# Weighted sums of the odd token tiles' expert outputs moved from VectorE to GpSimd in a four-layer transformer kernel

## What is computed

```python
# layer 2: 32 experts, 4 per token
topk_w, topk_idx = jax.lax.top_k(probs, 4); topk_w = topk_w / sum(topk_w)
act = jax.nn.silu(g) * u
eo = jnp.einsum('tei,eih->teh', act, w_down)
routed = jnp.einsum('te,teh->th', combine, eo)
...
# layer 3: 16 experts, 2 per token
for e in range(16):
    y = y + (silu(xf @ W1[e] + b1[e]) * (xf @ W11[e] + b11[e]) @ W2[e] + b2[e]) * gates[:, e, None]
```

## Time and profile before

| | us |
|---|---|
| median of 3 runs (lowest, highest) | 1688.22 (1686.22, 1691.62) |
| the profiled execution, its own time | 1694.55 |
| its span in the trace | 1692.7 |
| DVE busy in the span | 1250.0 (74%) |
| PE busy | 1260.5 (74%) |
| POOL busy | 412.5 (24%) |
| combine stage of layer 2: first gather issued, last combine begun | 1098.49, 1217.90 |
| combine stage of layer 3, the same | 1608.36, 1663.30 |

### The profile page before, as it was taken

The page is one execution under the profiler, slowest core; times in us unless marked ns, Lnnn a source line. Parts: engine busy times, 40 slices in busy tenths (PEclk is TensorE's granted clock), DMA queues, the critical chain, the costliest instruction groups (busy, mean ns, idle before and its releaser), DMA issues.

```text
span 1692.7 us, 24051 instructions
## 1 busy us (share of the span) xinstructions
PE 1260.5 (74%) x7110; PEld 675.0 (40%) x7198; DVE 1250.0 (74%) x4139; ACT 910.8 (54%) x2172; POOL 412.5 (24%) x578
## 2 busy tenths in 40 slices
PE   6988979887422333246678999977899888999976
PEld 2444544444111111131135656513366344666621
DVE  5998979989789999868656566667766865555672
ACT  3898988887254444411344565544444444455454
POOL 0111202002000000003556345265310153232160
PEclk7999989999755555555789999978899999999998
DMA  3010100100293000012332566333211026547220
GB/s 114 26 68 8 49 27 26 55 0 1 80 330 116 3 9 11 1 39 90 114 99 83 180 186 191 100 86 67 55 32 31 35 79 159 158 123 179 98 69 21
DMA packets 141387, 135.41 MB, mean 80 GB/s; under 512 B 75218, under 2 KB 114455, under 8 KB 141203
## 3 DMA queue, kind: packets, MB, share of 16 engines
q1 hardware_dynamic: 126185, 101.99, 20.6%
q0 software_dynamic: 13440, 31.48, 6.1%
q10 hardware_dynamic: 1632, 0.39, 0.1%
HBM read 95.96 MB, written 47.27 MB: 85 GB/s over the span
## 4 chain that ended last, share of the span: by engine, by line
PE 45%; DVE 33%; ACT 9%; issue 8%; another core or an unknown queue 2%; DMA 2%; SPq 1%; POOL 0%; DVEq 0%; ACTq 0%
PE PS L577 40%; DVE RA L1733 6%; DVE nmx L1488 5%; DVE RA L1737 4%; PE PS L573 4%; DVE RA L1291 3%; DVE RA L1294 2%; ACT RA L1879 1%; ACT RA L1929 1%; DVE RB L1291 1%; DVE RB L1294 1%; DVE X L1475 1%; DVE Otok L1218 1%; ACT RB L1885 1%
## 5 line engine op out<-in xcount | busy, mean ns | idle before, releaser
L577 PE MATMUL PS<-RA 128*128 128x512 bf16 (+6 forms) x1961 | 508.3, 352 | 102.4 <-DVE nmx L1488 64.6
L1488 DVE TENSOR_REDUCE nmx<-PS 128x1 f32<-128x512 f32 x512 | 347.2, 686 | 237.2 <-PE PS L577 210.0
L1929 ACT ACTIVATE RA<-PS 128x512 f32<-128x512 f32 x512 | 301.1, 599 | 214.9 <-PE PS L577 151.4
L577 PEld LDWEIGHTS PS<-RA 128*128 128x128 bf16 (+4 forms) x2048 | 200.7, 121 | 356.3 <-issue 142.1
L577 PE MATMUL PS<-RA,Vs 128*32 128x512 f32 x1240 | 204.1, 654 | 5.1 <-ACT RA L1929 1.0
L2055 ACT ACTIVATE RA<-RA 128x8 f32<-128x8 f32 x511 | 107.5, 210 | 143.0 <-DVE RA L1733 142.7
L573 PE MATMUL PS<-ident,RB 128*128 128x128 f32 (+2 forms) x331 | 62.7, 334 | 158.5 <-DVE RB L1666 142.9
L1908 ACT ACTIVATE RA<-PS 128x256 f32<-128x256 f32 (+1 forms) x144 | 55.0, 382 | 171.7 <-PE PS L577 158.3
L1291 DVE TENSOR_SCALAR RA<-PS 128x1024 f32<-128x1024 f32 x96 | 117.0, 1219 | 20.9 <-PE PS L577 20.6
L1879 ACT ACTIVATE RA<-RA,nm 128x512 f32<-128x512 f32 x192 | 128.8, 725 | 0.9 <-POOL nm L2225 0.7
L1294 DVE CUSTOM_DVE_ANT_0 RA<-RA,RB 128x512 f32<-128x512 f32 x192 | 125.1, 689 | 3.3
(11 more groups left out here) (312 smaller groups left out, 2127.1 us busy)
## 6 DMA issues: line engine op xcount, KB each, us to landing
RA<-scr SPq DMA_DIRECT2D x288, 96.0 KB
RA<-wd SPq DMA_DIRECT2D x28, 384.0 KB
xd<-Otok SPq DMA_DIRECT2D x36, 256.0 KB, 3.3
RA<-xd POOLq DMA_DIRECT2D x72, 128.0 KB, 3.8
RA<-wd SPq DMA_DIRECT2D x56, 160.0 KB
RB<-wd SPq DMA_DIRECT2D x20, 384.0 KB
RB<-wd SPq DMA_DIRECT2D x40, 160.0 KB
scr<-parts SPq DMA_DIRECT2D x48, 128.0 KB
```

What stands on the lines that cost most here:

```text
L577: return e.matmul(o, l, r, start=first, stop=last)
L1488: e.tensor_reduce(nmx[:, (g + lx) % 3, c:c + 1], bank[(6, 0)[i % 2]], AX.X, ALU.max, negate=True).then_inc(*ROWMAX.up(layer, n, i))
L1929: e.activation(chunk(layer, k, i), bank[(1, 5)[i % 2]], ACT.Exp).then_inc(*EXP.up(layer, k, i))
```

## The change

The combines of the odd tiles (n = 1, 3, ..., 15) are done by GpSimd; those of the even tiles stay on VectorE as they are. GpSimd has no single operation for it here, so it multiplies the gathered slot in place by the weight (a tensor_scalar) and, after a wait for its own result, adds the product to X[:, n] (a tensor_tensor). A new semaphore, `XR`, counts GpSimd's combines; `writer` picks `XW` or `XR` by the tile's parity wherever somebody waits for a combine: the gather i for slot i-6, VectorE's statistics and its later additions to X, the first row loads of layer 3, and the stores of the output. GpSimd keeps a `written` table of its own.

```diff
+    def writer(n, event):
+
+        return XR if event[0] == "routed" and n % 2 else XW
...
         def x_last(n):
             if n in written:
-                dve.wait_ge(XW, *written[n])
+                dve.wait_ge(writer(n, written[n]), *written[n])
...
             elif name == "combine":
                 i = task[1]
                 n, j = i // topk[lx], i % topk[lx]
-                dve.wait_ge(GATH[i % 6], lx, i)
-                x_last(n)
-                dve.wait_ge(ROUTE, "done", lx)
-                e.scalar_tensor_tensor(out=X[:, n, :], in0=XG[:, i % 6 // 2, i % 2, :], scalar=WJ[:, n, j:j + 1], in1=X[:, n, :],
-                                       op0=ALU.mult, op1=ALU.add).then_inc(*XW.up("routed", lx, i))
+                if n % 2 == 0:
+                    dve.wait_ge(GATH[i % 6], lx, i)
+                    x_last(n)
+                    dve.wait_ge(ROUTE, "done", lx)
+                    e.scalar_tensor_tensor(out=X[:, n, :], in0=XG[:, i % 6 // 2, i % 2, :], scalar=WJ[:, n, j:j + 1], in1=X[:, n, :],
+                                           op0=ALU.mult, op1=ALU.add).then_inc(*XW.up("routed", lx, i))
                 written[n] = ("routed", lx, i)
...
                 if i >= 6:
-                    pool.wait_ge(XW, "routed", lx, i - 6)
+                    pool.wait_ge(writer((i - 6) // k, ("routed",)), "routed", lx, i - 6)
...
+            elif name == "combine":
+                i = task[1]
+                n, j = i // k, i % k
+                if n % 2:
+                    pool.wait_ge(GATH[i % 6], lx, i)
+                    pool.wait_ge(writer(n, written[n]), *written[n])
+                    pool.wait_ge(ROUTE, "done", lx)
+                    y = XG[:, i % 6 // 2, i % 2, :]
+                    e.tensor_scalar(y, y, WJ[:, n, j:j + 1], None, ALU.mult).then_inc(*XR.up())
+                    pool.wait_last(XR)
+                    e.tensor_tensor(X[:, n, :], X[:, n, :], y, ALU.add).then_inc(*XR.up("routed", lx, i))
+                written[n] = ("routed", lx, i)
```

More of the change, by code:

```diff
@@ L268, in build @@
     XG_A, YO_A = signal("act_xg"), signal("act_yo")
-    ROOT = signal("pool_root")
+    ROOT, XR = signal("pool_root"), signal("pool_routed")
     SET, PARTS_P, BIAS_P, NEGMAX = signal("pool_set"), signal("pool_parts"), signal("pool_bias"), signal("pool_negmax")
@@ L2074, in pool_program @@
         e = pool.e
+        written = {}
         def early3(name, b, *more):
@@ L2149, in expert_step @@
                 if i >= 6:
-                    pool.wait_ge(XW, "routed", lx, i - 6)
+                    pool.wait_ge(writer((i - 6) // k, ("routed",)), "routed", lx, i - 6)
                 e.indirect_dma_start(XG[:, i % 6 // 2, i % 2, :], None, yd[lx],
                                      bass.IndirectOffsetOnAxis(ap=IDX[:, n, j:j + 1], axis=0)).then_inc(*GATH[i % 6].up(lx, i))
+            elif name == "combine":
[10 more added lines that the diff above has]
+                written[n] = ("routed", lx, i)
+            elif name == "down":
+                written[shared[lx][task[1]][0]] = ("shared", lx, task[1])
         def scatter(lx, i):
@@ L2165, in first_rows @@
             if lx:
-                pool.wait_ge(XW, "routed", 0, 16 * topk[0] - 1)
+                pool.wait_ge(XR, "routed", 0, 16 * topk[0] - 1)
             for u in range(6):
@@ L2209, in beside_step @@
                 biases()
+            for task in side[layer].get((n, i), ()):
+                if task[0] == {2: "proj2", 3: "proj"}[layer]:
+                    for tile in range(4 * task[1], 4 * task[1] + 4):
+                        written[tile] = ("x", layer, task[1])
         e.memset(Vs[:, :, :, :], 0.0).then_inc(*SET.up("vs"))
@@ L2475, in sp_program @@
             sp.wait_ge(XW, "shared", 1, 8 * b + 7)
-            sp.wait_ge(XW, "routed", 1, 8 * b + 7)
+            sp.wait_ge(XW, "routed", 1, 8 * b + 5)
+            sp.wait_ge(XR, "routed", 1, 8 * b + 7)
             e.dma_start(out[b].rearrange("(n p) d -> p n d", p=128), X[:, 4 * b:4 * b + 4, :]).then_inc(*STORE.up("all"))
```

## The result

The changed kernel took 1704.97 us (median of 5 runs, 1702.55 to 1708.44), the kernel before 1688.22 (5 runs, 1684.98 to 1691.62): a ratio of 1.0087, 95% interval 1.0068 to 1.0105; the medians differ by 16.8 us. I had forecast 1690.1 and no measurable change. The measured median lies 2 us above the upper end of my range, 1703 (by the ratio, 1.0087 x 1688.22 = 1702.9, it lies at that end), and comes out near the rival "GpSimd bounds both stages" (1701.0). The profiled execution took 1708.44 us, with a span of 1706.6.

A forecast was written before the change was run, and what follows sets the result against it. TensorE and VectorE bound the kernel by handing PSUM banks to and fro; with the change GpSimd bounds layer 3. Layer 2 -2.5, layer 3 +2.4 and blocking +2 gave +1.9 us on 1688.22: 1690.1, range 1681 to 1703.

The forecast's parts named there:

- GpSimd bounds both stages: Layers 2 and 3: at 1.2 us a combine GpSimd's queue costs +4.2 and +6.6, blocking 2: 1701.0 us; chance 0.22.
- the price of GpSimd's multiply: GpSimd's odd combines: a 128-column multiply takes 286 ns, drawn from the slope of its one-input casts.
- The two-level picture: Both combine stages: GpSimd works in order, and VectorE's even combine i waits for gather i to land.
- layer 3 has no room: Layer 3's stage: gather 29 lands at 1662.5, after combine 29's former 1660.10; +2.4 us, VectorE's gain not seen.
- the 2 of blocking: VectorE operations beside GpSimd's combines hold each other up; +2 us on the chain, between 0 and 4.
- The pair 0.85: GpSimd's multiply and add lengthen the distance of two gathers by 0.85 us, from 0.70 and two waits of 0.07.
- Landing: Both stages: a gather takes at most 4.4 us from issue to landing; 4.4 was taken.
- The burst wait: Layer 2: gathers 10 and 11 come behind combines 4 and 5, so VectorE waits 1.9 us at combine 11.
- VectorE's relief: Layer 2: 32 fewer combines on VectorE give 5.1 us, the chain's figure, capped at 4.9 by gather 59.
- The statistics: VectorE's statistics that wait for GpSimd's combines have one to two steps of room; 0.5 us put on them.
- the lock: Both engines' combines coincide by rhythm; half of 96 operations wait 0.2, 9.6 us on the chain: 1697.7 us; chance 0.08.
- What would show it: Signs in the changed trace: GpSimd nearly never idle, VectorE waiting before even combines, combine 59 earlier, combine 29 later.

The follow-up runs named there:

- its halves: Two kernels, GpSimd doing odd combines in only one layer, against the kernel before (1642.50 us): layer 2 only 1665.44 us, layer 3 only 1658.67 us.

## Why the prediction's mechanism held and its size did not

The forecast was +1.9 us and no measurable change; +16.8 was measured. That the range nearly reaches this is owed to its upper end, where every term stood at its largest together, and not to the sum. The step that failed is the price of GpSimd's multiply, and the smaller ones follow it.

- **The two-level picture** (GpSimd works in order, a gather behind its combines, an even combine behind its gather) was right, and so was the claim that layer 3 has no room. The rival's 1701.0 came from 1.2 us a combine; 1.24 was measured, 0.04 x 26 + 0.04 x 12 = 1.5 us more. The prediction's own working with 1.24 in the place of 0.85 lands gather 59 at 1215.5 and gather 29 at 1667.2, +5.2 and +7.1 us, with the 2 of blocking +14.3.
- **The multiply was mis-sized, and this decided the sign.** I drew 286 ns for 128 columns from a cast's slope between 512 and 1024 columns; it took 626, and 574 with a constant. The fit was right for what it fitted: the trace of before has casts of 128x128 at 288 and 291 ns. Wrong was to carry it over to another operation. That trace also had a float32 tensor_scalar of GpSimd, which I didn't read, with two columns only:

```profile
L2219 POOL CAST identb<-ident 128x128 bf16<-128x128 f32 x1 | 0.3, 288 | 0.0
L2225 POOL TENSOR_SCALAR nm<-mx 128x2 f32<-128x2 f32 x128 | 27.3, 213 | 319.0 <-DVE mx L1294 255.4 <-ACT RA L1879 55.1 <-ACT RB L1879 8.6
```

  It gives no price for 128 columns by itself, but 213 ns for two left only 73 for the other 126 in a price of 286. The add was right: 430 drawn from the slope, 450 to 476 measured. Of the seams 0.02 and 0.19 were taken, 0.04 and 0.27 measured. The pair 0.85, measured 1.24, over my own limit of 1.04 for a net loss in layer 2. The nearest whole row, the power operation's 0.96, lay nearer than the fit by chance only: it is one operation over 4 columns, not a pair over 128.
- **Landing.** I took 4.4 us. Gather 10 landed at most 4.38 us behind its issue (1115.30 to 1119.68), gather 11 5.67 (1117.80 to 1123.47), gather 29 of layer 3 2.67 (1670.79 to 1673.46). The burst wait that I had named, at combines 10 and 11, came, at 4.4 us for 1.9, and a third one of 5.3 which I had not. The nine waits of layer 3 (14.6 us) are the bound that I had forecast there.
- **VectorE's relief** was put at 5.1 us, capped at 4.9, and didn't show where the combines were dropped (ratios 1.0027 and 1.0022). It may be part of the 6 us by which the kernel that only adds beat the kernel before; no run tells the relief from the spacing of the gathers. The earlier trace rows gave 10.0% of the chain to "another core or an unknown queue", and I read past it. Half of a chain's share is what a cut gives only if nothing stands ready behind it.
- **The statistics** got 0.5 us. They waited three times, 9.4 us, once for 5.74:

```profile
1137.68 0.29 DVE L1538 BATCH_NORM_STATS2 st<-X 128x6 f32<-128x128 f32 x1 [5.74 <-POOL X L2169]
```

  They read a block of four tiles right behind its last, an odd one, so they meet GpSimd's row at its latest point. With the multiply doubled it was 8.99. That this is a cost on top of the row isn't shown: VectorE would have waited for a landing soon after.
- **Blocking** was put at 2 us and is of that size. The kept combines have 356 ns instead of 342 on average, some 0.49 beside GpSimd's work (1119.68 above), and GpSimd's add went up to 1.25 beside an operation of VectorE over 1024 columns with two inputs in SBUF:

```profile
1161.99 1.22 DVE L1191 TENSOR_TENSOR parts<-QK,parts 128x1024 bf16<-128x1024 f32 x1
1162.28 1.25 POOL L2169 TENSOR_TENSOR X<-X,RA 128x128 f32<-128x128 f32 x1
```

  A gather's issue beside another such operation (1157.01) took 1.63 us for 0.95. Over the stages that makes 48 x 0.014 = 0.7 us on VectorE, and 48 x (0.476 - 0.45) = 1.2 on GpSimd, the engine that bounds, if all of the difference is blocking. The rule of the Trainium skill (SBUF — State Buffer, Who interferes with whom), as the prediction has it, agrees in kind with these rows; what it cost is about a tenth of the loss. One of the prediction's rows was misread: the 0.17 us "where nothing ran beside it" (795.76) ran beside GpSimd's cast of 795.61 to 795.89, so it shows a tensor_scalar that a cast did not hold. The rival "the lock" (9.6 us) is not what happened.
- **What would show it**, in its own words: GpSimd busy to the end (102.1 of 128.2 us, before 66.2 of 119.4) and VectorE waiting before combines 10 and 11 were seen; combine 59 "two to three us earlier" was 9.1 later, combine 29 "some 2 later" 6.0. The granted clock fell from 0.87 to 0.84 in 40 us of layer 2's stage, with TensorE 29.5 instead of 31.6 us busy, and over the whole stages from 0.84 to 0.81 and from 0.91 to 0.86. All three signs that I had named for being wrong came: the pair over 1.0, the statistics waiting several us, the clock outside 0.87 to 0.89. The stretches, as in the earlier trace rows, and the two stages:

```profile
1140.00:1180.00 40.00, 29.54 (x140) 12.05 (x135) 27.48 (x70) 15.95 (x34) 33.04 (x40) 0.84 0.30 62
1097.80:1226.00 128.20, 89.66 (x415) 30.41 (x423) 79.35 (x212) 50.48 (x99) 102.09 (x127) 0.81 0.29 69
1615.80:1676.00 60.20, 43.13 (x195) 11.05 (x197) 35.06 (x83) 26.95 (x49) 45.67 (x59) 0.86 0.22 58
```

  Whether the lower clock added to the loss or only followed from TensorE's waiting, no run separated.

The change in all: 1.24 us for each of 48 combines on an engine that works in order, to spare another one 0.26. TensorE did wait for that other one before (for row maxima, 19.7 us in layer 2's stage and 8.3 in layer 3's), but with the change GpSimd's row was the longer one, and the relief couldn't count. No kernel that computes all outputs beat the kernel before.

## What to carry to other kernels

Before work goes to an engine that issues transfers, add up that engine's row with the new work in it, and compare it with the stage, not with the engine's busy share: GpSimd was busy 24% of the span and had, by the table's first line, 25 and 6 us of room in the two stages, for 35 and 15 us of new work. Price an operation from a row of the same operation, even of another shape; a fit over another operation is a guess, here of half the true length. And when a chain has a share that the profile cannot name, look up in the program what the engine waits for there: here it was TensorE, and what stopped TensorE is still open.

## What the runs showed of the hardware

- A GpSimd tensor_scalar over 128x128 float32 takes longer than a tensor_tensor of the same shape: 626 ns with a weight per partition, 574 with a constant, 476 for the add. ScalarE does the same product in 399.
- Gathers of 128 rows go out from GpSimd 1.26 us apart and landed 2.67 to 5.67 us behind their issue. With 0.49 us of an add between half of them the kernel was 8 to 11 us faster than without any add, and with room for fourteen in a row it was 32 us slower than with six slots (ratio 1.0185). Why isn't shown.
- The same kernel took 1642.5 us in one group of runs and 1686 to 1691 in the others. Where it took longer, TensorE stood up to 2.6 to 4.7 us at a time in front of a matmul without a wait that the profile shows, one of them at the same place of the program in all ten traces; where it was short, it stood 0.6 at most. The change's cost differed with it (39 us by its halves against 17 and 21). A comparison holds for the conditions in which it was made.
